# Weighted sums of two steps in one run, probabilities of three steps kept, input and residual in one buffer

## What is computed

```
x: [8, 32, 32, 192] f32
x = x + attention(groupnorm(x))     # 12 heads of 16, 1024 tokens per image, w_qkv, w_o
x = x + mixer(groupnorm(x))
attention: softmax(q k^T / 4) v per image and head, then @ w_o
mixer(x): bias = x @ bias_w.T + bias_b
          xf = rfft2(x) per 4 blocks of 48 channels
          two complex block matmuls (relu after the first), irfft2
          return that + bias
groupnorm: 32 groups of 6 channels over the image, no weights
```

## Time and profile before

| | |
|---|---|
| median of 3 runs | 1496.27 us (1491.05 to 1497.83) |
| profiled execution | 1497.2 us, span 1495.3 us |
| busy PE, PEld, DVE, ACT, POOL | 1425.8, 683.4, 1158.1, 1009.6, 187.5 us |
| DMA | 106.37 MB, mean 71 GB/s |

### The profile page before, as it was taken

One profiled execution on the slowest core, in us unless ns is written; L12 is line 12 of the kernel. 1 busy time (PEld: TensorE's weight loads), 2 busy tenths in 40 slices (PEclk: granted clock), 3 DMA queues, 4 the chain that ended last, 5 costly groups with the idle time before them and its releaser, 6 DMA issues.

```text
span 1495.3 us, 27421 instructions
## 1 busy us (share of the span) xinstructions
PE 1425.8 (95%) x9986; PEld 683.4 (46%) x9986; DVE 1158.1 (77%) x2155; ACT 1009.6 (68%) x2018; POOL 187.5 (13%) x277
## 2 busy tenths in 40 slices
PE   7699989899999999999999999999999999999988
PEld 4344333444545454444445454444545454434455
DVE  3687888788798878998798878998799978988041
ACT  1055777577776777677776777677777777677712
POOL 2000000130010300130010400121000400030000
PEclk7789999999999999999999999999999999999999
DMA  4430312313323414413322414413323324311213
GB/s 115 75 65 2 86 33 60 63 55 79 86 70 72 97 52 82 108 48 83 88 65 68 103 50 89 107 42 79 87 56 67 98 55 88 86 50 45 62 43 87
DMA packets 100463, 106.37 MB, mean 71 GB/s; under 512 B 24745, under 2 KB 77417, under 8 KB 100329
## 3 DMA queue, kind: packets, MB, share of 16 engines
q1 hardware_dynamic: 98616, 103.19, 30.1%
q10 hardware_dynamic: 1712, 1.43, 0.4%
HBM read 26.99 MB, written 6.67 MB: 23 GB/s over the span
## 4 chain that ended last, share of the span: by engine, by line
PE 79%; DVE 7%; DMA 6%; POOL 2%; issue 2%; SPq 2%; ACT 1%; ACTq 0%; DVEq 0%; POOLq 0%
PE o_acc L1288 21%; PE ring L1267 15%; PE scores L1235 14%; PE ring L1311 10%; DVE row_max L1033 5%; DMA inv_all<-inv_rows 4%; PE ring L1300 3%; PE ring L1424 2%; PE ring L1411 2%; PE ring L1417 2%; PE ring L1403 2%; PE scores L1311 1%; SPq L703 1%; POOL inv_all L577 1%; PE ring L1322 1%
## 5 line engine op out<-in xcount | busy, mean ns | idle before, releaser
L1033 DVE TENSOR_REDUCE row_max<-ring 128x1 f32<-128x512 f32 x1536 | 974.8, 682 | 181.6 <-PE ring L1267 175.2
L930 ACT ACTIVATE probs<-scores 128x512 f32<-128x512 f32 x1536 | 828.8, 600 | 271.1 <-PE scores L1235 270.2
L1267 PE MATMUL ring<-k_stack,q_stack 48*128 48x512 f32 x1536 | 589.1, 465 | 27.5 <-DVE row_max L1033 24.9
L1235 PE MATMUL scores<-q_stack,k_stack 50*128 50x512 f32 x1536 | 594.2, 460 | 2.6 <-DMA q_stack<-shift 1.3
L1288 PE MATMUL o_acc<-probs,v_aug 128*18 128x512 f32 x3072 | 407.5, 603 | 2.4 <-ACT probs L930 1.2
L1235 PEld LDWEIGHTS scores<-q_stack,k_stack 50*128 50x128 f32 x1536 | 244.0, 186 | 317.6 <-ACT probs L930 300.5
L1267 PEld LDWEIGHTS ring<-k_stack,q_stack 48*128 48x128 f32 x1536 | 246.1, 188 | 147.1 <-DVE row_max L1033 99.2
L577 POOL TENSOR_TENSOR inv_all<-o_raw,inv_all 128x1024 f32<-128x1024 f32 x23 | 54.5, 2371 | 585.8 <-DMA inv_all<-inv_rows 585.8
L1288 PEld LDWEIGHTS o_acc<-probs,v_aug 128*18 128x18 f32 x3072 | 51.9, 96 | 123.2 <-issue 87.8
L1311 PE MATMUL ring<-xt,w_qk 64*128 64x256 f32 x504 | 62.3, 379 | 0.0
L1311 PEld LDWEIGHTS ring<-xt,w_qk 64*128 64x128 f32 x504 | 48.8, 186 | 9.0 <-DVE row_max L1033 3.8
(11 more groups left out here) (158 smaller groups left out, 1097.8 us busy)
## 6 DMA issues: line engine op xcount, KB each, us to landing
q_stack<-qk_parts SPq DMA_DIRECT2D x288, 64.0 KB, 2.2
k_stack<-qk_parts SPq DMA_DIRECT2D x144, 128.0 KB, 4.2
inv_all<-inv_rows SPq DMA_DIRECT2D x23, 512.0 KB
rows_b<-rows_a SPq DMA_DIRECT2D x122, 96.0 KB, 2.8
x_in<-in_x_dram SPq DMA_DIRECT2D x8, 768.0 KB, 5.0
x_res<-in_x_dram SPq DMA_DIRECT2D x8, 768.0 KB, 4.7
spec_b<-spec_a SPq DMA_DIRECT2D x60, 102.0 KB, 2.3
o_t<-inv_all SPq DMA_DIRECT2D x184, 32.0 KB, 1.9
```

The source lines that it names most:

```text
L930: nc.scalar.activation(probs[:, GH * (s % 2) + h, :], scores[:, n % SCORE_BANKS, :], ACT.Exp, scale=SCALE).then_inc(probs_made, 1)
L1033: nc.vector.tensor_reduce(row_max[:, which, m:m + 1], max_bank(g, unit, i), AX.X, ALU.max).then_inc(max_taken, 1)
L1235: mm(scores[:, n % SCORE_BANKS, :], k_stack[rows, 2 * g + hp, P * kt:P * (kt + 1)], q_stack[rows, g, half, hp, :], start=True, stop=True). ...
L1267: mm(max_bank(g, unit, i), q_stack[rows, g, half, hp, P * qt:P * (qt + 1)], k_stack[rows, 2 * g + hp, HALF * which:HALF * (which + 1)], st ...
```

## The change

The weighted sums of the steps s - 2 and s - 1 run one after the other in every even step s, none in an odd step. `probs` keeps three steps (`KEPT`), and the first exponential of step s waits for the sum of step s - 3. ScalarE's copy of the second half of `o_acc` comes after the fourth exponential of step 0 and no longer after the second. `x_res` is the same buffer as `x_in`: the residual of image b - 1 is loaded in body b at step 5, after the turns of image b + 1, and the next input at step 19, after the last proj. The spread of the inverse is issued at step 4. The tables that place pieces, followers, copies of v and stacks are new.

```diff
+KEPT = 3
...
-    4: ([('turn', 2)], []),
+    5: ([], [('turn', 2)]),
-    23: ([('qk', 3)], []),
+    21: ([('qk', 3)], []),
...
-    14: ([('turn', 0)], []),
-    15: ([('turn', 1)], []),
-    16: ([('turn', 2)], []),
-    18: ([('mean', 0)], []),
+    14: ([('turn', 0), ('turn', 1)], []),
+    15: ([('turn', 2)], []),
+    17: ([('mean', 0)], []),
-    22: ([('spread', 0)], []),
+    23: ([('spread', 0)], []),
-    27: ([], [('dftw', 2)]),
-    28: ([('dftw', 3)], []),
-    29: ([('lin', 0)], []),
-    30: ([], [('dfth', 0), ('dfth', 1)]),
-    31: ([('dfth', 2)], []),
-    33: ([('dfth', 3), ('dfth', 4), ('dfth', 5)], []),
+    27: ([('dftw', 2)], [('dftw', 3)]),
+    29: ([('lin', 0)], [('dfth', 0)]),
+    31: ([('dfth', 1)], [('dfth', 2)]),
+    33: ([('dfth', 3), ('dfth', 4)], [('dfth', 5)]),
-    35: ([('mix1', 1)], []),
-    36: ([('lin', 1)], []),
-    37: ([('mix1', 2)], []),
-    38: ([('mix1', 3), ('mix1', 4), ('mix1', 5), ('mix1', 6), ('mix1', 7)], []),
-    40: ([('mix2', 0), ('mix2', 1)], []),
-    41: ([('mix2', 2), ('mix2', 3)], []),
+    35: ([('mix1', 1)], [('lin', 1)]),
+    37: ([('mix1', 2), ('mix1', 3)], []),
+    38: ([('mix1', 4), ('mix1', 5), ('mix1', 6)], []),
+    39: ([('mix1', 7)], []),
+    40: ([('mix2', 0)], []),
+    41: ([('mix2', 1), ('mix2', 2)], [('mix2', 3)]),
-    44: ([('lin', 2)], []),
-    45: ([('idfth', 0), ('idfth', 1), ('idfth', 2)], []),
-    46: ([('idfth', 3)], []),
+    44: ([('lin', 2)], [('idfth', 0), ('idfth', 1)]),
+    45: ([], [('idfth', 2), ('idfth', 3)]),
-    53: ([('idftw', 0)], []),
-    54: ([], [('idftw', 1)]),
+    53: ([('idftw', 0), ('idftw', 1)], []),
-PREP_FOLLOW = {0: [('stats', 0)], 3: [('stats', 1)], 6: [('stats', 2)], 7: [('gather', 0)], 12: [('normalise', 0)], 13: [('normalise', 1)], 14: [('normalise', 2)]}
-POST_FOLLOW = {14: [('stats', 0)], 15: [('stats', 1)], 16: [('stats', 2), ('gather', 0)], 26: [('normalise', 0), ('normalise', 1)], 27: [('normalise', 2)]}
-PLACE_V_AT = {26: 2, 40: 0, 45: 1}
-TOKENS_AT = {20: (0,), 21: (1,), 24: (2,), 27: (3,), 28: (4,), 30: (5,)}
-STACK_AT = {10: 'q1', 11: 'q0', 13: 'k'}
+PREP_FOLLOW = {1: [('stats', 0)], 3: [('stats', 1)], 5: [('stats', 2)], 7: [('gather', 0)], 13: [('normalise', 0), ('normalise', 1)], 15: [('normalise', 2)]}
+POST_FOLLOW = {13: [('stats', 0)], 14: [('stats', 1)], 16: [('stats', 2), ('gather', 0)], 25: [('normalise', 0), ('normalise', 1)], 26: [('normalise', 2)]}
+PLACE_V_AT = {32: 2, 38: 0, 41: 1}
+TOKENS_AT = {20: (0,), 22: (1,), 24: (2,), 26: (3,), 28: (4,), 29: (5,)}
+STACK_AT = {8: 'q0', 12: 'q1', 15: 'k'}
-SPREAD_AT = 5
+SPREAD_AT = 4
-RESIDUAL_AT = 17
-LOAD_AT = 3
+RESIDUAL_AT = 5
+LOAD_AT = 19
...
-        probs = sb("probs", [P, 2 * GH, HALF])
+        probs = sb("probs", [P, KEPT * GH, HALF])
-        x_res = sb("x_res", [P, NT, C])
+        x_res = x_in
...
+        def probs_at(g, s, h):
+            return GH * ((STEPS * g + s) % KEPT) + h
+
...
             def load_x(b):
+                if b > 2:
+                    post_taken(sp, b - 3, "proj", 7)
                 sp.dma_start(x_in[:, :, :], image(x, b)).then_inc(x_loaded, 16)
             def load_residual(b):
-                if not isinstance(b, int) or b > 0:
+                if b < NB - 2:
+                    sp.wait_ge(prep_made, N_PREP * (b + 2) + PREP_NO["turn", 2] + 1)
+                if b > 0:
                 sp.dma_start(x_res[:, :, :], image(x, b)).then_inc(x_res_loaded, 16)
...
-                    if u == RESIDUAL_AT:
+                    if u == RESIDUAL_AT and post:
+                        load_residual(b - 1)
+                    if u == LOAD_AT and b + 2 < NB:
+                        load_x(b + 2)
+                    if u == LOAD_AT and b == NB - 1:
-                    if u == LOAD_AT and prep and (not isinstance(b, int) or b + 2 < NB):
-                        load_x(b + 2)
...
                 act.wait_ge(scores_made, NG * TILES * b + n + 1)
-                    after(act, pv_made, STEPS * NG * b + STEPS * g + s - 1)
-                nc.scalar.activation(probs[:, GH * (s % 2) + h, :], scores[:, n % SCORE_BANKS, :], ACT.Exp,
+                    after(act, pv_made, STEPS * NG * b + STEPS * g + s + 1 - KEPT)
+                nc.scalar.activation(probs[:, probs_at(g, s, h), :], scores[:, n % SCORE_BANKS, :], ACT.Exp,
...
                     exponentials(b, g, s, 1)
-                    if s == 0 and not (first and g == 0):
-                        take_o(slot - 1, 1)
                     exponentials(b, g, s, 3)
+                    if s == 0 and not (first and g == 0):
+                        take_o(slot - 1, 1)
             def tail():
...
                 for h in range(GH):
-                              probs[:, GH * (s % 2) + h, :], start=(kt == 0), stop=(kt == NT - 1),
+                              probs[:, probs_at(g, s, h), :], start=(kt == 0), stop=(kt == NT - 1),
...
                     score_tile(b, g, s, 1)
-                    if s > 0:
-                        pv(b, g, s - 1)
-                    elif g > 0:
-                        pv(b, g - 1, STEPS - 1)
-                    elif not first:
-                        pv(b - 1, NG - 1, STEPS - 1)
+                    if s % 2 == 0 and not (first and u == 0):
+                        of = (b, g, s) if s else (b, g - 1, STEPS) if g else (b - 1, NG - 1, STEPS)
+                        pv(of[0], of[1], of[2] - 2)
+                        pv(of[0], of[1], of[2] - 1)
                     pieces(u, MID)
...
             def tail():
+                pv(NB - 1, NG - 1, STEPS - 2)
```

## The result

The changed kernel takes 1607.62 us (median of 3 runs, 1602.14 to 1609.25) against 1496.27: the ratio is 1.073, its 95% interval 1.069 to 1.078. It is 111 us slower, and outside the range of the prediction.

What follows compares the result with a forecast made beforehand. TensorE, busy 95%, was taken as the bound, with a ScalarE loop in empty steps. Gaps 124.1 plus 24 pairs of 1.86 gave 168.8 us per image, 169.9 with additions; 1497.2 + 6 x 0.3 + 2 = 1501, stated as 1499, range 1455 to 1530.

Steps and rivals of the forecast that it cites:

- The join: Two weighted sums in one run on TensorE: 1.86 us instead of 1.97, TensorE's work 6.7 us less per image.
- Rival D: At the joined sums: the second starts 0.54 us after the first's half, 19 us more, 1518; chance 0.08.
- The empty cycle: Two steps without a piece, from pair to pair: 5.43 us against 5.32 before, slower by 0.11.
- the last score product before the pair needs the exponential of three before it: Loop of TensorE and ScalarE through three score banks: sets the gap of 3.57 us in a cycle without pieces.
- a lone turn: Two steps with one turn as only piece: 6.19 us against 6.04, the piece costing nearly its whole length.
- rival B: In cycles with pieces: they hide where scores lie ahead, the saving arrives, range 1443 to 1482 us; chance 0.30.
- VectorE adds its own limit: Before even steps 10, 12, 32, 44: the last maximum product waits for six reductions, a gap of 4.73 us.
- rival **C: VectorE runs dry during the pair and ends late: 27 us more over 17 cycles per image, 1526; chance 0.17.
- I expect no change: TensorE's clock: granted in full in nearly all full images before, expected to stay so; no time added.
- I add 1 to each: Images 0 and 7, at 157.6 and 155.6 us: more empty cycles, so 1 us more for each.
- The pieces at their new steps: The 24 gaps of an image, from TensorE's piece lengths: 124.1 us, with 24 pairs of 1.86 168.8 us.
- Denominators and shared buffer: Copy about 2.4 us later, yet proj's DMA waits of some 6.7 us gone; shared buffer costs 0, at most 1 per image.

Runs made afterwards that it cites:

- a2: the changed kernel with the join undone, one sum in every step again and all else as changed: 1552.16 us, ratio 1.036 to the kernel before.
- b1: the changed kernel with the three normalisations of the second part one step later: 1588.63 us, ratio 1.060 to the kernel before.
- a5: the kernel before with input and residual in one buffer and its loads moved, nothing else: 1494.03 us, ratio 0.997.
- a1: the kernel before with the join, third probabilities buffer, later copy and shared buffer, on the old tables of pieces: 1621.73 us, ratio 1.083.
- c4: the kernel before with every row-maximum reduction over 256 of 512 columns: 1454.25 us, ratio 0.970.
- g1: a1 with every row-maximum reduction over 256 of 512 columns: 1499.83 us, ratio 1.001 to the kernel before.
- c2: the changed kernel with every row-maximum reduction over 256 of 512 columns: 1518.36 us, ratio 1.013 to the kernel before.
- a3: the changed kernel with a filler product before the third score product of each odd step: 1628.29 us, ratio 1.088 to the kernel before.
- d2: a2 with the three normalisations of the second part one step later: 1529.30 us, ratio 1.020 to the kernel before.

## Why the prediction was wrong

**The join, right.** The second sum streams: 1.84 us from the pair's start to the next product in the empty cycle, 1.86 forecast. Rival D is ruled out by it.

**The empty cycle, right in size, half right in cause.** 5.58 against 5.43; in the prediction's list of gaps the same cycle, from step 2, has 3.8, so 5.66. Its last waits are for row_max, so the step "the last score product before the pair needs the exponential of three before it" was not what closed it: halved exponentials leave it at 5.58. With halved reductions it takes 5.41, so the count of the loop over ScalarE was right, and VectorE's was 0.17 longer. A cycle with a lone turn (from step 14) takes 6.22 against the forecast's 6.2: a lone piece does cost nearly its whole length, so the sign of rival B didn't show.

**The body, mis-sized.** 24 cycles at the full clock, median of images 1 to 6, against gap + 1.86 of the forecast. For 12 of the 24 the forecast is within 0.2; nine are shown:

| cycle from step | before | a2 | after | forecast |
|---|---|---|---|---|
| 2 | 6.04 | 5.32 | 5.58 | 5.66 |
| 6 | 7.50 | 6.98 | 6.48 | 6.5 |
| 12 | 7.02 | 7.78 | 8.32 | 7.7 |
| 18 | 6.91 | 6.92 | 7.28 | 6.66 |
| 20 | 6.12 | 6.68 | 7.63 | 6.2 |
| 26 | 7.42 | 10.45 | 9.62 | 7.6 |
| 28 | 6.05 | 7.10 | 7.02 | 6.5 |
| 30 | 7.92 | 7.17 | 7.31 | 6.86 |
| 40 | 7.36 | 8.42 | 8.31 | 8.26 |
| all 24 | 169.1 | 174.7 | 176.9 | 168.8 (169.9 with the additions) |

The 8.1 us between 168.8 and 176.9 lie in few cycles, 5.6 of them in six: 2.0 in cycle 26 (GpSimd, b1), 1.4 in 20, 0.6 each in 12 and 18, 0.5 each in 28 and 30. What failed there is the step **"VectorE adds its own limit"**: I applied it in front of four even steps only, with reductions and nothing else. But VectorE also has statistics, copies and normalisations, and in a joined cycle it can work off at most the four finished products of the ring during the pair, since TensorE brings no new one for 1.84 us. That is rival **C**, with its sign right and its price (27 us) too low: its deciding amount "more than 0.4 us of other VectorE work" is met in 21 of the 24 cycles, and the join loses 82 us to the reductions by a5, a1, c4 and g1, clock included. The amount alone doesn't decide, though: the cycle from step 6 has 2.3 us of other VectorE work and came out as forecast, the one from step 20 has 1.0 and lost 1.4. Of that 1.4, 0.9 go with short reductions (6.70 in c2), and half a microsecond is there in a2 too, without the join; what delays the reductions there was not looked for.

**The clock, missing.** "I expect no change" was read from windows of full images at 0.99 to 1.00. The change took the sum, the only long work between thin products, out of every odd step, and waits for reductions fall into the same stretches. It came to 30 falls and, by the estimate from the rows, 52 us, the largest single term, with no range of its own. That the missing sums are behind the falls is supported by a3 (30 falls to 11) and, for the cycle from step 18, contradicted. Nothing in the trace of before was a row for it; a bound could have been had from the two falls of before, by asking what stood in front of them.

**Images 0 and 7, mis-sized.** "I add 1 to each" was 19.5 and 19.2. By the low clock 16 and 12 of that are the clock's. An image without pieces of its neighbour has the longest stretches of thin products; that this is the reason was not tested.

**The tables, mis-judged.** The count gave 168.8 for join and tables together, and no step asked what the tables do alone. They cost 51 to 58 us with single sums. The step at fault is in "The pieces at their new steps": it counts TensorE's pieces, and I moved GpSimd's and VectorE's followers at no cost, though a follower moved by one step can meet another engine's work; b1 and d2 show 19 and 23 us for it, part of them the clock's. It accounts for a third of what the tables cost; the rest is open.

**Denominators and shared buffer, right.** a5 is 4 us faster than the kernel before beside it, the waits of proj for DMA are gone and no new one came. The third probabilities buffer costs no time by itself as far as the empty cycle shows, which ends on a reduction; it wasn't run alone.

**The rule on PSUM's readers, right and used too weakly.** The Trainium skill's "TensorEngine Tiling (Array Packing)", PSUM Bottleneck, says that packing speeds up TensorE but not the reading of PSUM, which may then be the limit. c2 and g1 agree: short reductions take 89 us off after and bring the join's cost from 128 to 46. I placed the reader at ScalarE; VectorE holds more, 5.0 us per image at the full clock against 2.7.

Of the versions with whole reductions and whole exponentials only a5, 1494.0, is faster than both kernels.

## What to carry to other kernels

Work that shares an engine with the products for two consumers is also their spacing: joining two pieces into one run saves the break, but it starves each consumer for the whole run, and the banks between them (here four, 0.62 us each, 2.5 us) bound what it can work off meanwhile. Before joining, count per cycle all of the consumer's work, not only the stream's, and what stands behind each wait. A table of followers is to be read against every engine's timeline of that step, and a stretch that will hold only thin products is to be asked for its clock.

## What the runs showed of the hardware

**A VectorE instruction beside GpSimd.** A tensor_scalar from SBUF to SBUF, 128x512 f32, takes 0.54 us and took up to 2.05 beside GpSimd's tensor_tensor of 1.8 to 2.0 us; the reductions, which read PSUM, did not lengthen (681 to 683 ns on average wherever they are whole). GpSimd's copy went from 0.62 (b1) to 0.81. The Trainium skill's "SBUF — State Buffer", Who interferes with whom, says that tensor_scalar can use a second port pair which one of the two engines holds for a whole instruction while the other is blocked, and that tensor_reduce never does. The trace agrees with both: of the two normalisations in the rows of the timeline, the first was issued 0.7 us into GpSimd's first addition and took 1.39, to 1085.72, some 0.2 after that addition's end; both together ended at 1087.68, 0.3 after the second addition's (1087.40).

**The clock.** It fell from 2.4 to 1.2 GHz in windows of whole images in which TensorE showed work for over 90% of the time (168.6 of 177.0 us, 177.6 of 184.9). The rows before the fall shown hold score and maximum products on 50 and 48 rows, one-column products, waits of 0.2 to 0.4 us, and no weighted sum. With 192 products of 128 rows that add nothing in the odd steps 30 falls became 11, and with short reductions 11 as well, but the cycle from step 18 fell in a3 no less than in after. Each us at 1.2 GHz lengthened a cycle by 0.45 us, and a2's runs give 0.41. Work that TensorE alone holds would lose half; that the waits for other engines make the difference is a reading and not shown.
